# Cross-attention and expert layer on one core: batch 2's normalized input turned on TensorE, with new program orders on every engine

## The chip, the core and the metric

The kernel runs on one core of one Trainium2 chip. Five engines work side by side, each through its own list of instructions in order: TensorE (PE, matmuls), VectorE (DVE), ScalarE (ACT), GpSimd (POOL) and SyncE (SP), which here only issues DMAs. They wait for each other on semaphores. The metric is the device time of one execution in microseconds; lower is better.

## The reference, cut to what matters

```python
B, S, H = 4, 512, 512; T = 64; NH = 16; HD = 32; E = 8; K = 2; I = 16     # all float32
hs = layernorm(x)
q = clean(hs @ Wq.T + bq); k = clean(ctx @ Wk.T + bk); v = clean(ctx @ Wv.T + bv)
scores = clip(q @ k.T / sqrt(HD), -50, 50)
scores = clip(where(mask > 0.5, scores, -10000), -50, 50)
probs = softmax(scores); probs = probs / (probs.sum(-1) + 1e-8)
delta = clip(residual_scale, 0, 0.3) * ((probs @ v) @ Wo.T + bo)
x1 = x + layernorm(delta) * ln_gamma + ln_beta
n = layernorm(x1)
weights = softmax(x1 @ router_w.T)          # 8 experts, the two largest kept
a = silu(n @ down_w.T)                      # 8 experts x 16
out = x1 + sum over experts(gate * (a @ up_w.T))
```

The router, too, works on the normalized x1.

## The kernel before

A batch b (0 to 3) is 512 rows, in four tiles t of 128 rows. The program is a list of small steps, written out by hand for each engine in the order in which the engine runs them; a step named with (b, t) works on one tile, with (b, c), (b, m) or (b, r) on one chunk of the 512 columns or of the heads, with (b, j) or (b, g) on half a batch. There is no scheduler: an engine that reaches a step whose semaphore is not there yet stands, and all behind it stands too.

The steps of TensorE, with their lines in the kernel before (all products of two float32 operands that need accuracy are run as three passes of a high and a low part):

- `keys(c)`, `values(c)` (L522, L532): K and V of the context, one chunk of the weights each. They need the cleaned context chunk, counted by `ctx_ok`.
- `hs_transpose(b, t)` (L489): the normalized tile `hs` turned into a PSUM bank (uses h..). ScalarE then writes the high part (`hs_hi`, L748), VectorE the low part (`hs_lo`, L1089), which frees the bank.
- `query(b, m)` (L471, `hst`, `wq`): 12 matmuls of 512 columns. `query(b, 0)` waits for all four low parts of the batch. `query_out` (L771, ACT) takes it off.
- `scores(b, r)` (L548), `exp_scores` (L784, ACT), `clip` (L1148, DVE: the limits and the mask).
- `sums(b, g)` (L562): the softmax sums, 8 rows of which `reciprocals` (L1153, DVE) inverts; `spread_out` and `spread_in` send them to DRAM and back, spread over the partitions, into `wk`.
- `weigh(b, g)` (L575): probs times V; `product` (L1158, DVE) multiplies by the spread reciprocals; `att_hi` (L802, ACT) and `att_lo` (L1510, POOL) split it.
- `project(b, t)` (L471, `attt`, `wo`): 12 matmuls onto a bank in which `seed` (L845, ACT) has put the bias. Waits for the whole batch's `att_lo`.
- `projected_squares` (L854, ACT), `residual_powers` (POOL), `scaled` (L1167, DVE), `residual` (L1175, DVE), `x1_squares` (L862, ACT), `x1_powers` (POOL): the two layer norms.
- `down(b, t)` (8 matmul records of 136 columns each pass), `hid_transpose(b, j)`, `up(b, t)`: the experts; between them `down_scaled`, `hidden_tanh`, `exp_logits` (ACT), `rivals` (POOL), `largest`, `gating`, `hid_lo` (DVE), and at the end `finish` (L1224, DVE) and `store` (SP).

There are two ways to turn a tile. On TensorE as above, or moved: VectorE turns blocks of 32x32 (`hs_turn`, L1106; `x1_turn`, L1114), and two DMAs, out to DRAM and back in, put the blocks in place (`hs_send`, `hs_fetch`; `x1_send`, `x1_fetch`). `MOVED_HS` names the batches whose hs is moved (2 and 3 before), `MOVED` the halves whose x1 is moved (batches 0 to 2). For a moved batch the low part `hs_lo` is GpSimd's (L1516), for the others VectorE's.

The eight PSUM banks are dealt by the table `BANKS`: each line is a bank and the uses that follow each other in it. `take` makes TensorE wait until the use ahead in the same bank is freed. So `h11` behind `h10`'s bank mate, or `v10` behind `h..`, ties steps together.

At the start TensorE runs `WARM` = 18 matmuls on a constant tile while the first inputs land. SP issues all DMAs from one queue, in its written order; ahead of `x1_load` it waits until all four context chunks are cleaned (`clean_wait`, since the later loads `experts_load` and `bv_load` write over scratch that the cleaning reads). `load(2)` waits for both values to be complete (x of batch 2 takes the place of the value weights), `load(3)` for `wo_low(3)` (it takes that of the output weights).

## Time and profile before

| what | value |
|---|---|
| median of 3 runs | 198.33 us (197.42 to 199.66) |
| the profiled execution, its own time | 198.77 us |
| its span, first to last instruction | 197.1 us |
| TensorE busy | 178.3 us, 90% of the span |
| VectorE busy | 143.6 us, 73% |
| ScalarE busy | 112.5 us, 57% |
| GpSimd busy | 104.5 us, 53% |
| mean granted TensorE clock | 0.963 |

A busy share near 90% says that TensorE has work nearly always; what is left is the time in which it stood, and the time in which it ran at the lower of its two clock levels (0.50 in the profile is 1.2 GHz, 1.00 is 2.4 GHz). Matmul records overlap at their ends, so the distance from start to start is what one costs, not its own length.

### The profile page before, as it was taken

To read this page: it belongs to the slowest core of one execution; us is meant where nothing else is said; L and a number is where in the kernel's file an instruction comes from. 1 tells how busy PE (TensorE), PEld (TensorE's weight loads), DVE (VectorE), ACT (ScalarE), POOL (GpSimd) and SP (SyncE) were. 2 spreads that over 40 slices of the span, in tenths; PEclk is the share of its full clock that TensorE was granted. 3 is DMA by queue.
4 is the path that set the end of the run, shared out by engine and by line. 5 is a ranking of instruction groups with operands and counts; after the bars stand their busy time and mean duration, and the time that the engine had idled before them with its cause. 6 is when DMAs were issued, how large, how long until landed. Compare 5 with 4: busy or idle time off the path is not lost. (4 is left out here: it accounts for less than half of the span.)

```text
span 197.1 us, 3587 instructions
## 1 busy us (share of the span) xinstructions
PE 178.3 (90%) x1228; PEld 130.7 (66%) x1228; DVE 143.6 (73%) x306; ACT 112.5 (57%) x231; POOL 104.5 (53%) x157
## 2 busy tenths in 40 slices
PE   7999999399993999999599999986999999999970
PEld 7777686258832587885286876663775977888840
DVE  2867799999845894056982606789698999678991
ACT  3038537778309685175666833589554868567500
POOL 4060035499969999388694111794244872472000
PEclk9999999969998599999889999999999999999998
DMA  5994994005694326773305401553434482002337
GB/s 165 358 388 143 292 398 181 0 7 226 176 254 147 78 91 190 174 192 127 110 0 189 139 10 39 192 211 110 119 106 157 155 276 73 0 2 106 136 130 271
DMA packets 18050, 30.14 MB, mean 153 GB/s; under 512 B 3056, under 2 KB 8176, under 8 KB 17776
## 3 DMA queue, kind: packets, MB, share of 16 engines
q1 hardware_dynamic: 18032, 29.92, 46.6%
q8 instruction: 10, 0.16, 0.3%
q14 instruction: 8, 0.07, 0.1%
HBM read 19.95 MB, written 9.96 MB: 152 GB/s over the span
## 5 line engine op out<-in xcount | busy, mean ns | idle before, releaser
L471 PE MATMUL ps<-hst_hi,wq_hi 128*128 128x512 f32 x64 | 27.4, 428 | 0.0
L471 PE MATMUL ps<-hst_hi,wq_lo 128*128 128x512 f32 x64 | 26.4, 413 | 0.0
L471 PE MATMUL ps<-hst_lo,wq_hi 128*128 128x512 f32 x64 | 26.4, 412 | 0.0
L471 PE MATMUL ps<-wo_hi,attt_hi 128*128 128x512 f32 x64 | 26.1, 407 | 0.0
L471 PE MATMUL ps<-wo_hi,attt_lo 128*128 128x512 f32 x64 | 25.3, 395 | 0.0
L471 PE MATMUL ps<-wo_lo,attt_hi 128*128 128x512 f32 x64 | 25.2, 394 | 0.0
L1510 POOL TENSOR_TENSOR attt_lo<-wk,attt_hi 128x512 fp32r<-128x512 f32 x16 | 23.3, 1471 | 1.5 <-ACT attt_hi L802 1.5
L1506 POOL TENSOR_TENSOR xs<-xs,beta_bc 128x512 f32<-128x512 f32 x16 | 21.4, 1366 | 2.2 <-DMA beta_bc<-beta 2.2
L862 ACT ACTIVATE cen<-xs,n_sum 128x512 f32<-128x512 f32 x16 | 11.5, 721 | 15.5 <-DVE xs L1175 15.5
L1148 DVE TENSOR_SCALAR stage<-stage,exp_max 128x1024 f32<-128x1024 f32 x16 | 19.0, 1205 | 2.0 <-ACT stage L784 1.8
L765 ACT ACTIVATE hs<-xs,ln_bias,ln_rstd 128x512 f32<-128x512 f32 x16 | 12.1, 808 | 13.2 <-POOL ln_bias L1498 13.2
L1525 POOL TENSOR_SCALAR d_ve<-d_sq,rs_sq 128x1 f32<-128x1 f32 x16 | 5.9, 366 | 25.8 <-ACT cen L854 25.4
L1153 DVE RECIPROCAL rz<-ps 128x128 f32<-128x128 f32 x8 | 7.5, 952 | 15.4 <-PE ps L562 15.4
L771 ACT ACTIVATE q_sb<-ps,bq_sb 128x512 f32<-128x512 f32 x16 | 10.9, 684 | 13.1 <-PE ps L471 13.1
L1167 DVE TENSOR_TENSOR cen<-ps,gamma_bc 128x512 f32<-128x512 f32 x16 | 10.8, 677 | 10.1 <-ACT cen L854 10.1
L1175 DVE SCALAR_TENSOR_TENSOR xs<-cen,d_rstd,xs 128x512 f32<-128x512 f32 x16 | 14.1, 882 | 5.3 <-POOL d_rstd L1528 4.7
L471 PEld LDWEIGHTS ps<-dr_raw,x1t 128*128 128x128 f32 x128 | 15.5, 190 | 2.9 <-issue 2.2
L471 PEld LDWEIGHTS ps<-hst_hi,wq_hi 128*128 128x128 f32 x64 | 13.0, 202 | 6.4 <-issue 2.0
L784 ACT ACTIVATE stage<-ps 128x1024 f32<-128x1024 f32 x16 | 15.7, 1020 | 2.4 <-PE ps L548 2.4
L471 PE MATMUL ps<-dr_raw,x1t 128*128 128x136 f32 x128 | 16.6, 282 | 0.3 <-ACT x1t L748 0.2
L471 PEld LDWEIGHTS ps<-wo_hi,attt_hi 128*128 128x128 f32 x64 | 12.0, 188 | 5.6 <-issue 2.9
L854 ACT ACTIVATE cen<-ps 128x512 f32<-128x512 f32 x16 | 9.5, 591 | 10.3 <-PE ps L471 10.2
(111 smaller groups left out, 396.9 us busy)
## 6 DMA issues: line engine op xcount, KB each, us to landing
wk<-rz_scratch SPq DMA_DIRECT2D x32, 128.0 KB, 2.7
out<-xs SPq DMA_DIRECT2D x16, 256.0 KB, 2.3
xs<-x SPq DMA_DIRECT2D x3, 1024.0 KB, 7.8
x_scratch<-x_turned SPq DMA_DIRECT2D x6, 512.0 KB, 2.6
x_turned<-x_scratch SPq DMA_DIRECT2D x24, 128.0 KB, 2.7
hs_scratch<-hs_turned SPq DMA_DIRECT2D x2, 1024.0 KB, 3.8
hs<-hs_scratch SPq DMA_DIRECT2D x8, 256.0 KB, 5.2
wk<-wk_t SPq DMA_DIRECT2D x4, 256.0 KB, 5.9
```

The lines of the kernel that those rows point to most:

```text
L471: last = pe.matmul(dst, w, m, start=start and i == 0, stop=stop and i == n - 1, skip_group_check=unseen)
L765: act.activation(hs[:, t, :], xs[:, bass.ds(tile, 1), :], ACT.Identity, bias=ln_bias[:, bass.ds(tile, 1)], scale=ln_rstd[:, bass.ds(tile, ...
L771: act.activation(q_sb[:, m, :], bank(f"Q{b}{m}"), ACT.Identity, bias=bq_sb[:, m:m + 1]).then_inc(q_ok, 1)
L784: act.activation(probs[:, 2 * c:2 * c + 2, :], bank(f"S{b}{2 * c}", 2).rearrange("p (c n) -> p c n", c=2), ACT.Exp, scale=SCALE).then_inc( ...
L854: act.activation(cen[:, t, :], bank(f"W{b}{t}"), ACT.Square, accum_out=d_sq[:, NT * b + t:NT * b + t + 1]).then_inc(d_sq_ok, 1)
L862: act.activation(cen[:, t, :], xs[:, bass.ds(NT * b + t, 1), :], ACT.Square, bias=n_sum[:, NT * b + t:NT * b + t + 1], scale=-float(H), ac ...
L1148: dve.tensor_scalar(probs[:, ps, :], probs[:, ps, :], EXP_LO, exp_max[:, b:b + 1], ALU.max, ALU.min).then_inc(probs_ok, 1)
L1153: dve.reciprocal(rz[:, g, :], bank(f"s{b}{g}")[:, 0:P]).then_inc(sums_out, 1)
L1167: dve.tensor_tensor(cen[:, t, :], bank(f"W{b}{t}"), gamma_rs[:, :], ALU.mult).then_inc(w_free, 1)
L1175: dve.scalar_tensor_tensor(x_tile, cen[:, t, :], d_rstd[:, NT * b + t:NT * b + t + 1], x_tile, ALU.mult, ALU.add, accum_out=n_sum[:, NT * ...
L1506: pool.tensor_tensor(xt, xt, beta_bc[:, :], ALU.add).then_inc(xb_ok, 1)
L1510: pool.tensor_tensor(attt_lo[:, :, c, :], att[:, c, :].rearrange("p (t n) -> p t n", t=NT), attt_hi[:, :, c, :].bitcast(F32), ALU.subtract ...
```

## The change

`MOVED_HS` loses batch 2: its four tiles are now turned by `hs_transpose(2, 0)` to `(2, 3)` on TensorE and their low parts made by VectorE; `hs_turn`, `hs_send` and `hs_fetch` of batch 2 and GpSimd's four `hs_lo(2, t)` are gone. hs of batch 3 and x1 of batches 0 to 2 stay moved. `WARM` is 10 instead of 18. `clean_wait` is gone; its wait now stands in `experts_load`, and `x1_load`, `gamma_load`, `wo_load` and `bo_load` are issued ahead of it. `keys(0)` runs ahead of `values(0)`. The tables of banks and the order of steps on all five engines are new from there to the end. `weigh` gets one more wait, for the clipped probs that it reads. No step computes anything else than before.

```diff
-WARM = 18
+WARM = 10
-MOVED_HS = (2, 3,)
+MOVED_HS = (3,)
...
             def experts_load():
+                sp.wait_ge(ctx_ok, KC)
...
             small_load()
-            clean_wait()
             x1_load()
+            gamma_load()
+            wo_load()
+            bo_load()
+            experts_load()
             bv_load()
-            experts_load()
-            wo_load()
             load(2)
-            gamma_load()
-            bo_load()
-            hs_send(2)
+            load(3)
             spread_out(0, 0)
             spread_in(0, 0)
-            hs_fetch(2)
-            load(3)
             spread_out(0, 1)
...
             x1_send(0, 1)
+            hs_send(3)
             x1_fetch(0, 1)
+            hs_fetch(3)
             spread_out(2, 0)
             spread_in(2, 0)
+            x1_send(1, 0)
+            x1_send(1, 1)
+            x1_fetch(1, 0)
+            x1_fetch(1, 1)
             spread_out(2, 1)
             spread_in(2, 1)
...
                 if b == 0:
                     pe.wait_ge(values_out, 2)
+                pe.wait_ge(probs_ok, KC * b + 2 * g + 2)
...
+            keys(0)
             values(0)
-            keys(0)
             values(1)
             keys(1)
...
             query(0, 3)
-            scores(0, 0)
             hs_transpose(1, 0)
             hs_transpose(1, 1)
             hs_transpose(1, 2)
+            scores(0, 0)
             hs_transpose(1, 3)
+            expert_means()
+            query(1, 0)
+            sums(0, 0)
             scores(0, 1)
-            sums(0, 0)
-            query(1, 0)
+            weigh(0, 0)
             query(1, 1)
+            sums(0, 1)
+            scores(1, 0)
             query(1, 2)
             query(1, 3)
-            sums(0, 1)
-            weigh(0, 0)
-            scores(1, 0)
             weigh(0, 1)
-            expert_means()
+            sums(1, 0)
             scores(1, 1)
+            hs_transpose(2, 0)
+            hs_transpose(2, 1)
+            hs_transpose(2, 2)
+            project(0, 0)
+            project(0, 1)
+            project(0, 2)
+            sums(1, 1)
+            hs_transpose(2, 3)
+            project(0, 3)
             query(2, 0)
             query(2, 1)
             query(2, 2)
```

TensorE, in the program behind the last matmul of `query(0, 3)`. L548 is `scores`, L489 `hs_transpose`, L562 `sums`, L471 on `hst` `query`. Before:

```order
L471 MATMUL ps<-hst_hi,wq_lo 128x512
L548 MATMUL ps<-q_sb,k_sb 64x512 x8
L489 MATMUL ps<-ident,hs 128x128 x16
L548 MATMUL ps<-q_sb,k_sb 64x512 x8
L562 MATMUL ps<-stage,sum_ones 32x128 x16
L471 MATMUL ps<-hst_hi,wq_hi 128x512
```

The same place now (the lines are 4 lower: L544 is `scores`, L485 `hs_transpose`; L467 on `average` is `expert_means`):

```order
L467 MATMUL ps<-hst_hi,wq_lo 128x512
L485 MATMUL ps<-ident,hs 128x128 x12
L544 MATMUL ps<-q_sb,k_sb 64x512 x8
L485 MATMUL ps<-ident,hs 128x128 x4
L467 MATMUL ps<-dr_raw,average 128x136 x4
L467 MATMUL ps<-hst_hi,wq_hi 128x512
```

The first scores moved between the third and the fourth transpose of batch 1, `expert_means` came forward to here, and `scores(0, 1)` and `sums(0, 0)` went behind `query(1, 0)`.

VectorE, from the statistics of batch 2's tiles to the low parts of batch 1 (L1232 and L1234 are `tile_stats`, L1148 `clip`, L1089 `hs_lo`, L1249 `scale_gamma`). Before:

```order
L1249 TENSOR_SCALAR gamma_bc<-gamma_bc,rs_sb 128x512
L1232 BN_STATS ln_st<-xs 128x6
L1234 BN_AGGR ln_mv<-ln_st 128x2
L1148 TENSOR_SCALAR stage<-stage,exp_max 128x1024
L1089 TENSOR_TENSOR hst_lo<-ps,hst_hi 128x512 x3
L1148 TENSOR_SCALAR stage<-stage,exp_max 128x1024
L1089 TENSOR_TENSOR hst_lo<-ps,hst_hi 128x512
L1106 STREAM_TRANSPOSE hs_turned<-hs 128x4x4x32 x4
```

Now (L1241 to L1245 are `centre_wo`, L1090 `hs_lo`, L1149 `clip`):

```order
L1241 BN_STATS w_st<-xs 128x6
L1243 BN_AGGR w_mv<-w_st 128x2
L1245 TENSOR_SCALAR xs<-xs,w_mv 128x512
L1090 TENSOR_TENSOR hst_lo<-ps,hst_hi 128x512 x4
L1241 BN_STATS w_st<-xs 128x6
L1243 BN_AGGR w_mv<-w_st 128x2
L1245 TENSOR_SCALAR xs<-xs,w_mv 128x512
L1149 TENSOR_SCALAR stage<-stage,exp_max 128x1024 x2
```

The four low parts of batch 1 stand together and ahead of the first clips, two of the tile statistics of batch 2 moved behind them, and the four turns of batch 2 are gone.

SyncE, from the last small load to the first `spread_out`. Before (L305 is x of batch 1, L330 bv, L333 to L335 the experts, L314 Wo, L347 x of batch 2):

```order
L321 DMA rs_raw<-rs 128x1
L305 DMA xs<-x 128x4x512
L330 DMA hidden<-bv 128x512
L333 DMA dr_raw<-down_t 128x4x128
L334 DMA dr_raw<-router_t 128x4x8
L335 DMA hidden<-up_t 128x512
L314 DMA xs<-wo_t 128x4x512
L347 DMA xs<-x 128x4x512
L338 DMA gamma_bc<-gamma 128x512
L339 DMA beta_bc<-beta 128x512
L324 DMA bo_bc<-bo 128x512
L367 DMA hs_scratch<-hs_turned 128x2048
```

Now:

```order
L321 DMA rs_raw<-rs 128x1
L305 DMA xs<-x 128x4x512
L337 DMA gamma_bc<-gamma 128x512
L338 DMA beta_bc<-beta 128x512
L314 DMA xs<-wo_t 128x4x512
L324 DMA bo_bc<-bo 128x512
L332 DMA dr_raw<-down_t 128x4x128
L333 DMA dr_raw<-router_t 128x4x8
L334 DMA hidden<-up_t 128x512
L328 DMA hidden<-bv 128x512
L346 DMA xs<-x 128x4x512 x2
L352 DMA rz_scratch<-rz 128x128
```

Gamma, beta, Wo and bo moved ahead of the experts and bv, both x loads stand together, and the send of batch 2's turned hs is gone.

## Rows read from the trace of the kernel before

**Rows 1.** The page: busy times, and the granted clock in 40 slices.
```profile
PE 178.3 (90%) x1228; PEld 130.7 (66%) x1228; DVE 143.6 (73%) x306; ACT 112.5 (57%) x231; POOL 104.5 (53%) x157
PEclk9999999969998599999889999999999999999998
```

**Rows 2.** Waits of TensorE: line, op <- releaser: total us, times, longest.
```profile
PE ps L548 <- ACT stage L784: 3.3, 1, 3.3
PE ps L489 <- DVE hst_lo L1089: 3.2, 1, 3.2
PE ps L575 <- DVE wk L1158: 2.1, 1, 2.1
PE ps L489 <- DVE hidden L1215: 1.9, 2, 1.6
```

**Rows 3.** Timeline of TensorE: start us, us, line, operation, count [idle before].
```profile
1.05 6.12 PE L624 MATMUL ps<-average 128*128 128x128 f32 x36 [1.05 <-POOL average L1563]
...
22.43 0.51 PE L471 MATMUL ps<-hst_hi,wq_hi 128*128 128x512 f32 x1
...
33.79 1.11 PE L548 MATMUL ps<-q_sb,k_sb 32*64 32x512 f32 x16
34.84 1.53 PE L489 MATMUL ps<-ident,hs 128*128 128x128 f32 x12
39.59 1.09 PE L489 MATMUL ps<-ident,hs 128*128 128x128 f32 x4 [3.23 <-DVE hst_lo L1089]
40.61 1.99 PE L548 MATMUL ps<-q_sb,k_sb 32*64 32x512 f32 x16
...
63.47 2.01 PE L548 MATMUL ps<-q_sb,k_sb 32*64 32x512 f32 x16 [3.29 <-ACT stage L784]
65.41 0.80 PE L471 MATMUL ps<-hst_hi,wq_hi 128*128 128x512 f32 x1
...
69.82 0.39 PE L471 MATMUL ps<-hst_lo,wq_hi 128*128 128x512 f32 x1
```

**Rows 4.** Timeline of TensorE again, around the third stop.
```profile
96.28 1.26 PE L575 MATMUL ps<-stage,v_sb 64*32 64x512 f32 x16 [2.13 <-DVE wk L1158]
97.46 0.79 PE L471 MATMUL ps<-hst_hi,wq_hi 128*128 128x512 f32 x1
...
100.56 0.39 PE L471 MATMUL ps<-hst_lo,wq_hi 128*128 128x512 f32 x1
```

**Rows 5.** Timeline of VectorE: cleaning, clips, and a product behind its spread.
```profile
4.86 0.45 DVE L1275 COPY_PREDICATED compare<-dr_raw,stage 128x256 f32<-128x256 uint8 x1
...
48.78 3.48 DVE L1148 TENSOR_SCALAR stage<-stage,exp_max 128x1024 f32<-128x1024 f32 x2
...
66.64 1.29 DVE L1158 TENSOR_TENSOR wk<-ps,wk 128x512 f32<-128x512 f32 x2 [0.47 <-DMA wk<-rz_scratch]
```

**Rows 6.** Groups by line: operation, count | busy us, mean ns | idle before.
```profile
L1510 POOL TENSOR_TENSOR attt_lo<-wk,attt_hi 128x512 fp32r<-128x512 f32 x16 | 23.3, 1471 | 1.5 <-ACT attt_hi L802 1.5
L1148 DVE TENSOR_SCALAR stage<-stage,exp_max 128x1024 f32<-128x1024 f32 x16 | 19.0, 1205 | 2.0 <-ACT stage L784 1.8
L1089 DVE TENSOR_TENSOR hst_lo<-ps,hst_hi 128x512 fp32r<-128x512 f32 x8 | 5.3, 686 | 2.5 <-ACT hst_hi L748 2.4
L1106 DVE STREAM_TRANSPOSE hs_turned<-hs 128x512 f32<-128x512 f32 x8 | 5.0, 672 | 0.0
```

**Rows 7.** SyncE's DMA issues: start us, us of issuing, line, transfer, count.
```profile
46.09 0.33 SPq L353 DMA_DIRECT2D rz_scratch<-rz  x1
49.26 1.72 SPq L361 DMA_DIRECT2D wk<-rz_scratch  x4
...
62.46 1.72 SPq L361 DMA_DIRECT2D wk<-rz_scratch  x4
```

**Rows 8.** Busy us of each engine (instructions) in one stretch, granted clock, DMA share, GB/s.
```profile
140.00:190.00 50.00, 49.37 (x320) 39.21 (x319) 42.80 (x120) 31.30 (x85) 21.73 (x42) 1.00 0.35 116
```

**Rows 9.** The last row of the chain that ended last: start us, us, what.
```profile
192.05 0.60 DVE xs L1224
```

More of the change, by code:

```diff
@@ new lines, in _ @@
+            x1_squares(0, 3)
+            query_out(2, 1)
+            query_out(2, 2)
+            x1_out(0, 0)
+            att_hi(1, 0)
+            att_hi(1, 1)
+            exp_scores(2, 0)
+            down_scaled(0, 0)
+            exp_scores(2, 1)
+            x1_out(0, 1)
+            att_hi(1, 2)
+            att_hi(1, 3)
+            query_out(2, 3)
+            x1_out(0, 2)
+            x1_out(0, 3)
+            seed(1, 0)
+            exp_scores(2, 2)
+            down_scaled(0, 1)
@@ L1342, in _ @@
             hs_lo(1, 2)
+            hs_lo(1, 3)
+            centre_wo(3)
+            clip(0, 0)
             clip(0, 1)
-            hs_lo(1, 3)
-            hs_turn(2, 0)
-            hs_turn(2, 1)
-            hs_turn(2, 2)
-            hs_turn(2, 3)
+            tile_stats(2, 2)
             reciprocals(0, 0)
-            centre_wo(2)
-            centre_wo(3)
+            tile_stats(2, 3)
             clip(0, 2)
+            centre_experts()
             clip(0, 3)
             centre_bo()
+            tile_stats(3, 0)
@@ L1367, in _ @@
+            clip(1, 2)
+            clip(1, 3)
+            hs_lo(2, 0)
             hs_turn(3, 0)
+            scaled(0, 0)
+            hs_lo(2, 1)
+            hs_lo(2, 2)
+            scaled(0, 1)
             hs_turn(3, 1)
             hs_turn(3, 2)
-            hs_turn(3, 3)
-            clip(1, 2)
-            clip(1, 3)
-            reciprocals(1, 0)
+            residual(0, 0)
             reciprocals(1, 1)
-            scaled(0, 0)
-            residual(0, 0)
-            x1_turn(0, 0)
@@ L1378, in _ @@
-            scaled(0, 1)
+            hs_lo(2, 3)
             residual(0, 1)
-            x1_turn(0, 1)
             scaled(0, 2)
             residual(0, 2)
+            scaled(0, 3)
+            x1_turn(0, 0)
+            x1_turn(0, 1)
+            x1_turn(0, 2)
+            residual(0, 3)
+            x1_turn(0, 3)
+            hs_turn(3, 3)
             product(1, 0)
             product(1, 1)
-            scaled(0, 3)
-            residual(0, 3)
-            product(1, 2)
             clip(2, 0)
@@ L1418, in _ @@
+            hid_lo(0, 0)
+            clip(3, 0)
+            clip(3, 1)
+            largest(0, 1)
+            gating(0, 1)
+            reciprocals(3, 0)
+            product(2, 2)
+            product(2, 3)
+            largest(1, 0)
             clip(3, 2)
             clip(3, 3)
-            largest(0, 1)
-            hid_lo(0, 0)
-            reciprocals(3, 1)
+            product(3, 0)
+            product(3, 1)
             scaled(2, 0)
             residual(2, 0)
-            gating(0, 1)
+            x1_turn(2, 0)
@@ L1426, in _ @@
             scaled(2, 1)
+            reciprocals(3, 1)
             residual(2, 1)
-            x1_turn(2, 0)
+            finish(0, 0)
+            finish(0, 1)
             x1_turn(2, 1)
+            gating(1, 0)
             hid_lo(0, 1)
             scaled(2, 2)
-            product(3, 0)
-            product(3, 1)
             residual(2, 2)
```

462 lines of the change are left out of this document (208 added, 254 removed), and 16 rows, old and new, of the table BANKS.

## The prediction

> **What bounds the kernel now.** The page comes first: TensorE is busy 178.3 of 197.1 us, and its granted clock falls in three places of the 40 slices [rows 1]. So the time is TensorE's work, plus the stretches where it stands, plus what the lower clock costs behind them. TensorE's waits name the stops: three of 3.3, 3.2 and 2.1 us, and two short ones of 1.9 us together [rows 2]. Its timeline shows where they lie and what follows each. I price them from start to start:
>
> - Full rate: `query(0, 0)` to `(0, 3)` take 22.43 to 33.79, 11.36 us for 48 matmuls, 0.237 us each; one `scores` takes 33.79 to 34.84, 1.05 us; twelve transposes take 1.53 us, 0.13 us each [rows 3].
> - Stop A: `hs_transpose(1, 3)` stands 3.23 us for VectorE's low part of tile (1, 0), whose bank it needs. The clock is then at its lower level (1.2 GHz): four transposes take 39.59 to 40.61, 1.02 for 0.52, and `scores(0, 1)` about 1.94 for 1.05 (that is what the other `scores` at this level takes, 63.47 to 65.41) [rows 3]. 3.2 + 0.5 + 0.9 = 4.6 us.
> - Stop B: `scores(1, 1)` stands 3.29 us for the exponentials, which on ScalarE are queued behind four `hs_hi(2, t)` that wait for batch 2's hs to come back from DRAM. Then the `scores` loses 0.9 us, and ten matmuls take 65.41 to 69.82, 4.41 for 2.37 [rows 3]. 3.3 + 0.9 + 2.0 = 6.2 us.
> - Stop C: `weigh(1, 1)` stands 2.13 us for a product, and seven matmuls then take 97.46 to 100.56, 3.10 for 1.66 [rows 4]. 2.1 + 1.4 = 3.6 us with rounding.
>
> Together 14.4 us, which an order that fits better can give back. From 140 to 190 us TensorE is busy 49.37 of 50 and VectorE 42.80 [rows 8]: little can be had there, and VectorE is close to being the bound itself.
>
> **The change, part by part.**
>
> *The beginning.* The warm-up with the 36 records of 18 matmuls runs from 1.05 for 6.12 us [rows 3]; the first context chunk is clean at 4.86 + 0.45 = 5.3 [rows 5]. Eight matmuls fewer end it at about 5.3, so TensorE starts `keys(0)` 1.7 us earlier. A few tenths are lost again, because the first transposes now come before ScalarE's second tile is ready. I take 1.4 us (bounds 0.8 and 1.7): `query(0, 0)` at 21.0 for 22.4. The earlier x1, gamma and Wo loads only keep this up: by my count VectorE ends the low parts of batch 0 at 20.8 and four statistics of 0.85 at 24.2; GpSimd, which first adds beta four times (1.4 us each, from about 19.5), has the scales at 27; ScalarE, between other steps, has the tiles normalized by 31.6, and TensorE asks for them at 32.3. That is little cover: GpSimd later by over 1 us shows on TensorE.
>
> *Stop A goes.* `scores(0, 0)` now stands between the third and fourth transpose, and the four low parts of 0.69 us [rows 6] ahead of the clips. The first is done at about 34.3, TensorE asks at 34.7. `query(1, 0)` needs the fourth, at about 36.7, and `expert_means` ends at 36.1: 0.6 us of new wait.
>
> *Stop B goes, clips and products come in its place.* ScalarE no longer waits for batch 2's round trip. But between `hs_lo(1, 3)` and `clip(1, 1)` VectorE has a `centre_wo`, six clips, six tile statistics, two reciprocals, `centre_experts`, `centre_bo`, gamma and two products. With clips at their mean of 1.2 us [rows 6] that is 18.9 us of work, and 0.8 of waits puts it at 56.3. TensorE in the same stretch has four queries (11.4), two `scores`, two `weigh`, two `sums` and short waits, and asks for `clip(1, 1)` at about 55.0. Two clips with GpSimd busy took 3.48 us, 1.74 each [rows 5]; at that price six of them are 3.2 us longer. I take 1.1 of it: the wait of `sums(1, 0)` is 2.4, and `sums(0, 0)` and `(0, 1)` wait 1.0 together (bounds 2.0 and 5.5 for the three).
>
> The Trainium skill (SBUF — State Buffer, "Who interferes with whom") says that a VectorE operation in a two-port mode and a GpSimd operation shut each other out for a whole instruction. The long clips agree. By that rule, with a GpSimd operation of about 1.4 us ahead of each clip, the six would cost some 8 us more and not 1.1, and the sum would come to about +1.
>
> *Transposes of batch 2.* Sixteen at 0.13 us are 2.0 us more on TensorE [rows 3]. VectorE gives four turns of 0.67 us for four low parts of 0.69 [rows 6], nothing; GpSimd loses four low parts; the send and four fetches leave SP's queue. The banks of these transposes hang on the products: h20 needs `product(0, 2)`, h21 `product(0, 3)`, h22 a reciprocal. A product comes 7.4 us after its reciprocal: 3.2 from the send to the fetch (46.09 to 49.26) and 4.2 from the fetch to the product (62.46 to 66.64) [rows 5, 7]. `reciprocals(0, 1)` ends at about 50.6 (36.6, then `centre_wo` 1.4, four clips 4.8, four statistics 3.4, two reciprocals 1.8, two centrings 2.0, waits 0.6), so `product(0, 2)` is at 58 to 59, and TensorE arrives at 58.4 to 59.5. Behind `product(0, 3)` come two `att_hi` of 0.6 and two `att_lo` of 1.47 us on GpSimd [rows 6] before `project(0, 0)` may start. I count 2.5 us here (bounds 1 and 5).
>
> *Stop C goes.* `weigh(1, 1)` finds its products made. In its place `down(0, 0)` stands right behind `scores(2, 0)` and needs x1 of batch 0 back from DRAM: about 0.9 us. Two more small ones, `weigh(2, 1)` behind `down_scaled` and `up(1, 0)` behind a low part, are 0.8.
>
> *The last third.* The short stops of 1.9 us [rows 2] go, since `hid_transpose(0, 0)` has more work ahead of it. TensorE arrives about 6 us earlier, but VectorE's work there is the same, and it was 86% busy [rows 8]: transposes and downs of batches 2 and 3 in turn wait for banks. I add 1.0 net (bounds 0 and 5). The tail from the last `finish` (192.05 + 0.60, then the store) [rows 9] stays at 4.5 us.
>
> *The clock.* Several waits now lie together between 55 and 62 us. Before, it fell after each of the three stops of over 2 us and after none of the short ones. I add 0.8 us, a third to a half of what it cost behind A, B or C (1.4 to 2.9).
>
> The sum: −1.4 (beginning) −4.6 −6.2 −3.6 (stops A, B, C) −1.9 (short stops) +2.0 (transposes) +0.6 +2.4 +1.0 +2.5 +0.9 +0.8 (new waits, 8.2) +0.8 (clock) +1.0 (last third) = −5.7 us. The span goes from 197.1 to 191.4. The profiled execution took 198.77, 0.4 above the median of 198.33; against the median the forecast is 192.6 us.
>
> **The rivals.**
>
> *More comes back.* If clips run at the mean and the last third keeps pace, 2.4 falls to 1.3, and the clock, last-third and part of the product terms vanish: 3 to 4 us more, about 189. For it: the new order has work ahead of each old stop. Against: VectorE's share at the end.
>
> *The clock falls in the new cluster, and clips are slow.* Then the waits at 55 to 62 cost 2.9 like B's clock loss and 2 us more of clips: +4, 196.6. The Trainium skill (TensorE: Matmul & The Clock Gate, "PE-mode transpose") says that transposes on TensorE do not count as busy for its clock gate; by that the twelve of batch 2, each behind a wait, would bring the clock down at `project(0, 0)`, with the same 196.6. Against it: the twelve at 34.84 ran at full rate, 0.13 us each [rows 3].
>
> *Slower: the reciprocals of batch 2 stuck in SP's queue.* `spread_out(2, 1)` is now behind two sends and eight fetches of x1 of batch 1, the second send waiting for `x1_turn(1, 3)`. From that turn it is 2.6 us for the send, 3.5 for the fetches, then 7.4 for the spread: 13.5 us until `product(2, 2)`, which frees the bank of `weigh(3, 0)`. TensorE has about 13 us of work between. So this place has no slack, and every us by which VectorE's turn is late is a us of standing, and 2 us for the clock on top. It decides from 6 us of lateness: −5.7 + 6 + 2 is 200.6, 1% above before. For it: VectorE is the bound of the first 60 us, too; against it: TensorE and VectorE slip together there.
>
> *Nothing changes:* the waits only move, all new ones at their upper bounds (+3, +2.5, +4) against −5.7: about 198 to 202.
>
> **How the numbers follow.** The forecast, 190 to 195.5 around 192.6, gets 0.55; more comes back (below 190) 0.15; clock and clips (195.5 to 197.5) 0.15; nothing changes (197.5 to 200.3) 0.06; the stuck queue or another late chain (above) 0.09. A measurement of this kernel tells 1% from no change, 196.35 to 200.31. Faster: 0.55 + 0.15 + half of 0.15 is 0.78; same 0.12; slower 0.10. The range that leaves out less than 2 in 10 is 188.5 to 198.0; the likeliest case's own is 190 to 195.5.
>
> **What would show it.** `query(0, 0)` starts at 21 us and `query(1, 0)` before 38. No stop of TensorE over 3 us; its waits name `clip`, products and `attt_lo` between 50 and 64 us, in all 4 to 7 us, and the granted clock falls at most once there. `project(2, 0)` starts some 7 us earlier than before. The transposes of hs are 48, at 0.13 us from start to start. I am wrong if the waits of the middle exceed 10 us, if ScalarE's order, which I followed only along TensorE's needs, holds a wait that I do not see, or if the last third loses more than 5 us to VectorE.

## The result and the profile after

The changed kernel takes 189.55 us (median of 4 runs, 189.04 to 191.93); before stands at 198.26 us in the same comparison. The ratio is 0.9545 [0.9475, 0.9616], 8.7 us less. The forecast was 192.6 us with 188.5 to 198.0, so the time lies in the range, but where the rival "more comes back" was put (below 190). The ratios, here and in the table below, leave out executions more than 1.5% above the fastest of the same kernel; the medians hold all of them.

The first profile of the changed kernel is of its longest execution, in which the clock fell twice. The rows below are of the same kernel, run again: 190.21 us, span 188.4, mean clock 1.000. On the page the busy time of TensorE and the granted clock in 40 slices answer to [rows 1]:

```profile
PE 173.6 (92%) x1228; PEld 127.4 (68%) x1228; DVE 140.2 (74%) x306; ACT 113.8 (60%) x231; POOL 98.8 (52%) x153
PEclk9999999999999999999999999999999999999999
```

TensorE's waits answer to [rows 2] (total us, times, longest):

```profile
PE ps L544 <- ACT q_sb L772: 1.7, 1, 1.7
PE ps L467 <- POOL attt_lo L1511: 1.3, 1, 1.3
```

Its timeline over the places of stops A and B and the new cluster answers to [rows 3] (L621 the warm-up, L528 `values`, L518 `keys`, L485 transposes, L544 `scores`, L558 `sums`, L467 the rest):

```profile
1.05 4.40 PE L621 MATMUL ps<-average 128*128 128x128 f32 x20 [1.05 <-POOL average L1564]
...
9.54 1.98 PE L528 MATMUL ps<-xs,compare 128*128 128x512 f32 x4 [0.65 <-DMA xs<-wv_t]
11.93 1.99 PE L518 MATMUL ps<-compare,wk 128*128 128x256 f32 x8 [0.41 <-DMA wk<-wk_t]
...
33.69 1.47 PE L485 MATMUL ps<-ident,hs 128*128 128x128 f32 x12
35.09 1.11 PE L544 MATMUL ps<-q_sb,k_sb 32*64 32x512 f32 x16
36.79 0.63 PE L485 MATMUL ps<-ident,hs 128*128 128x128 f32 x4 [0.58 <-DVE hst_lo L1090]
37.29 1.19 PE L467 MATMUL ps<-dr_raw,average 128*128 128x136 f32 x8
38.96 0.47 PE L467 MATMUL ps<-hst_hi,wq_hi 128*128 128x512 f32 x1 [0.48 <-DVE hst_lo L1090]
...
42.53 1.08 PE L558 MATMUL ps<-stage,sum_ones 128*32 128x128 f32 x32 [0.54 <-DVE stage L1149]
...
58.60 1.11 PE L544 MATMUL ps<-q_sb,k_sb 32*64 32x512 f32 x16
60.17 1.22 PE L485 MATMUL ps<-ident,hs 128*128 128x128 f32 x8 [0.46 <-DVE wk L1159]
61.64 0.63 PE L485 MATMUL ps<-ident,hs 128*128 128x128 f32 x4 [0.24 <-DVE rz L1154]
63.52 0.47 PE L467 MATMUL ps<-wo_hi,attt_hi 128*128 128x512 f32 x1 [1.25 <-POOL attt_lo L1511]
```

The fourth transpose of batch 1 waits 0.58 us where stop A was 3.23. `scores(1, 1)` at 58.60, where stop B was, and `weigh(1, 1)`, where stop C was, do not wait at all. The waits in front of `project(0, 0)` are 0.46, 0.24 and 1.25, and the clock stays at 1.00 behind them.

**Where the 8.7 us are.** The profiled spans are 197.1 and 188.4. TensorE's busy time fell by 4.7 us (178.3 to 173.6). That is 1.7 less warm-up (6.12 to 4.40), 2.1 more for the 16 transposes, and so, by difference, 5.1 for the lower clock that is gone. The stops inside TensorE's list, those of over 0.15 us added up, fell from 11.7 to 9.4: −2.3. From TensorE's last matmul to the end it was 5.95 us and is 4.09: −1.9, and of this 1.6 is the last stores of that one execution of before, which landed late. The last `finish` ended 4.45 us before the end there and 2.8 to 2.9 us before it in the experiments on before below. So TensorE's part is about 7 us in this pair, and the clock is the larger share of it. The medians are 8.7 us apart as well, but each profiled execution is slower than its median, by 0.5 and 0.7 us, and the late stores belong to one execution; so about 1.6 us of the difference of the medians is not in this account and stays open.

Times and clocks of single executions give a second estimate. In 27 executions of before, the mean clock went from 0.952 (spans 197.2 to 199.2) to 0.989 (194.5). A straight line through them gives 0.97 us per 0.01, and 193 at full clock; single executions lie up to 2.2 us off it. The changed kernel has 0.996 or more in seven of its eight executions. By that line about 3 us of the 8.7 are clock, by the busy times above 5; I take it as 3 to 5. That is an estimate: an execution that stands longer also has the lower clock, so the line cannot tell the two apart.

### The profile page after: what moved, and what is told of

Its sections match the earlier page's. It is cut to its first block, busy times and chain, and to the rows that moved or that the text cites. A ratio compares the mean times of both kernels' runs of the same rounds, so it can differ in the third digit from the quotient of the medians.

```text
span 190.1 us, 3580 instructions
## 1 busy us (share of the span) xinstructions
PE 176.2 (93%) x1228; PEld 128.9 (68%) x1228; DVE 140.2 (74%) x306; ACT 113.9 (60%) x231; POOL 98.6 (52%) x153
## 4 chain that ended last, share of the span: by engine, by line
PE 15%; DMA 13%; DVE 12%; issue 6%; SPq 5%; ACT 4%; POOL 4%; DVEq 0%; ACTq 0%
PE ps L467 11%; DMA x_scratch<-x_turned 4%; DMA wk<-rz_scratch 4%; DMA x_turned<-x_scratch 3%; SPq L381 3%; DVE xs L1225 3%; DMA rz_scratch<-rz 2%; PE ps L572 2%; POOL d_rstd L1529 2%; DVE x_turned L1115 2%; SPq L360 1%; PE ps L544 1%; DVE xs L1176 1%; PE ps L558 1%; DVE cen L1168 1%
## 5 line engine op out<-in xcount | busy, mean ns | idle before, releaser
L1511 POOL TENSOR_TENSOR attt_lo<-wk,attt_hi 128x512 fp32r<-128x512 f32 x16 | 20.3, 1282 | 17.4 <-ACT attt_hi L803 17.4
L467 PE MATMUL ps<-wo_hi,attt_hi 128*128 128x512 f32 x64 | 25.9, 405 | 1.2 <-POOL attt_lo L1511 1.2
L467 PE MATMUL ps<-hst_hi,wq_hi 128*128 128x512 f32 x64 | 26.5, 414 | 0.3 <-DVE hst_lo L1090 0.3
L467 PE MATMUL ps<-hst_lo,wq_hi 128*128 128x512 f32 x64 | 25.7, 402 | 0.0
L467 PE MATMUL ps<-hst_hi,wq_lo 128*128 128x512 f32 x64 | 25.4, 397 | 0.0
L467 PE MATMUL ps<-wo_hi,attt_lo 128*128 128x512 f32 x64 | 25.3, 395 | 0.0
L467 PE MATMUL ps<-wo_lo,attt_hi 128*128 128x512 f32 x64 | 25.2, 394 | 0.0
L467 PEld LDWEIGHTS ps<-dr_raw,x1t 128*128 128x128 f32 x128 | 15.6, 190 | 3.8 <-issue 2.7
L467 PE MATMUL ps<-dr_raw,x1t 128*128 128x136 f32 x128 | 16.5, 282 | 0.6 <-DVE hidt_lo L1090 0.4
L863 ACT ACTIVATE cen<-xs,n_sum 128x512 f32<-128x512 f32 x16 | 11.5, 722 | 9.2 <-DVE xs L1176 9.1
L772 ACT ACTIVATE q_sb<-ps,bq_sb 128x512 f32<-128x512 f32 x16 | 10.9, 683 | 10.1 <-PE ps L467 10.0
L1149 DVE TENSOR_SCALAR stage<-stage,exp_max 128x1024 f32<-128x1024 f32 x16 | 14.3, 922 | 3.5 <-ACT stage L785 3.5
L467 PEld LDWEIGHTS ps<-hst_hi,wq_hi 128*128 128x128 f32 x64 | 12.4, 194 | 6.0 <-issue 2.7
L1159 DVE TENSOR_TENSOR wk<-ps,wk 128x512 f32<-128x512 f32 x16 | 10.3, 682 | 8.0 <-PE ps L572 4.2
L1176 DVE SCALAR_TENSOR_TENSOR xs<-cen,d_rstd,xs 128x512 f32<-128x512 f32 x16 | 13.2, 828 | 3.1 <-POOL d_rstd L1529 2.8
L803 ACT CAST attt_hi<-wk 128x512 fp32r<-128x512 f32 x16 | 9.7, 616 | 9.4 <-DVE wk L1159 7.3
L467 PEld LDWEIGHTS ps<-wo_hi,attt_hi 128*128 128x128 f32 x64 | 12.0, 188 | 4.2 <-issue 1.8
L467 PEld LDWEIGHTS ps<-hst_hi,wq_lo 128*128 128x128 f32 x64 | 12.3, 193 | 2.9
L467 PEld LDWEIGHTS ps<-hst_lo,wq_hi 128*128 128x128 f32 x64 | 12.3, 193 | 2.5
```

What stands on the lines that cost most here:

```text
L467: last = pe.matmul(dst, w, m, start=start and i == 0, stop=stop and i == n - 1, skip_group_check=unseen)
L772: act.activation(q_sb[:, m, :], bank(f"Q{b}{m}"), ACT.Identity, bias=bq_sb[:, m:m + 1]).then_inc(q_ok, 1)
L803: act.copy(attt_hi[:, :, c, :], att[:, c, :].rearrange("p (t n) -> p t n", t=NT)).then_inc(attt_hi_ok, 1)
L863: act.activation(cen[:, t, :], xs[:, bass.ds(NT * b + t, 1), :], ACT.Square, bias=n_sum[:, NT * b + t:NT * b + t + 1], scale=-float(H), ac ...
L1149: dve.tensor_scalar(probs[:, ps, :], probs[:, ps, :], EXP_LO, exp_max[:, b:b + 1], ALU.max, ALU.min).then_inc(probs_ok, 1)
L1159: dve.tensor_tensor(att[:, c, :], bank(f"v{b}{c}"), att[:, c, :], ALU.mult).then_inc(weighed_out, 1)
```

## The experiments

The first four run or edit the changed kernel, the next four edit the kernel before, the last four the changed kernel again. Medians are of 4 runs (one of 10); before is 198.7, 198.3 and 197.5 us in the three groups. A dash says that no ratio is on record.

| kernel | us | ratio to before |
|---|---|---|
| changed, again | 189.47 (188.06 to 190.43) | 0.9537 [0.9464, 0.961] |
| changed, hs of batch 2 moved | 196.63 (192.21 to 198.49) | – |
| changed, transposes of batch 2 twice | 189.70 (189.46 to 191.33) | 0.9572 [0.9507, 0.9636] |
| changed, WARM 18 | 189.76 (188.53 to 190.24) | 0.9547 [0.9486, 0.9609] |
| before, low parts first | 200.83 (199.4 to 201.12) | 1.0154 [1.007, 1.0238] |
| before, fetch first | 196.58 (193.62 to 198.21) | – |
| before, both | 200.06 (199.3 to 201.23) | 1.0135 [1.0042, 1.0228] |
| before, WARM 10 | 195.49 (193.91 to 198.2) | 0.9872 [0.9758, 0.9986] |
| changed, query_out first | 189.47 (189.21 to 190.1) | 0.9613 [0.9554, 0.9672] |
| changed, load(3) later | 192.80 (191.71 to 194.59) | 0.9756 [0.9692, 0.982] |
| changed, all three | 193.74 (191.29 to 196.62) | 0.9741 [0.9653, 0.9829] |
| changed, moved, filled | 196.71 (193.77 to 198.51) | 0.986 [0.9801, 0.992] |

### The changed kernel again

> The changed kernel again, as the yardstick of this chip for the three runs beside it. Both theories: 189.5 us, within 0.7 us. Its traces so far had stops of TensorE of 2.0 us ahead of scores(3, 0) and 1.9 us ahead of hs_transpose(1, 3); where the clock falls behind them it is 2 us longer.

189.47 us; its rows are above. The time repeats.

### hs of batch 2 moved again

```diff
-MOVED_HS = (3,)
+MOVED_HS = (2, 3,)
...
             spread_out(0, 1)
             spread_in(0, 1)
+            hs_send(2)
             spread_out(1, 0)
+            hs_fetch(2)
             spread_in(1, 0)
...
-            hs_transpose(2, 0)
-            hs_transpose(2, 1)
-            hs_transpose(2, 2)
             project(0, 0)
...
-            hs_transpose(2, 3)
             project(0, 3)
```

with the low parts of batch 2 still VectorE's, and the steps of batches 2 and 3 on ScalarE, VectorE and GpSimd put where the new order has room.

> The changed kernel with hs of batch 2 turned by VectorE and two DMAs again, its low parts still VectorE's; hs_norm(3), hs_hi(2), hs_lo(2) and hs_turn(3) had to be put where this leaves no circle of waits. Theory of the order (the gain is that of stops removed by new orders, and the transposes themselves only cost TensorE 2.0 us): 187.5 to 189.5 us, since the round trip of 12 us fits behind project(0, 0) to (0, 2). Rival, the gain comes from the round trip that is no longer there: 192 us or more, with a stop of over 2 us ahead of query(2, 0).

196.63 us, 7.2 more in the median. All four executions (192.21 to 198.49) lie above all of the changed kernel's, so it is slower; how much by is less sure. The rival's time has come, but not its place: the stop ahead of `query(2, 0)` is 0.62 us, not over 2. TensorE's timeline, and two 5-us stretches (busy us of PE, PEld, DVE, ACT, POOL, then clock, DMA share, GB/s):

```profile
63.60 0.76 PE L469 MATMUL ps<-wo_hi,attt_hi 128*128 128x512 f32 x1 [3.66 <-POOL attt_lo L1513]
...
79.15 0.47 PE L469 MATMUL ps<-hst_hi,wq_hi 128*128 128x512 f32 x1 [0.62 <-DVE hst_lo L1096]
...
92.80 2.15 PE L469 MATMUL ps<-dr_raw,x1t 128*128 128x136 f32 x8 [2.73 <-ACT x1t L809]
```
```profile
60.00:65.00 5.00, 1.40 (x3) 1.16 (x4) 3.81 (x5) 4.84 (x8) 2.49 (x2) 0.68 0.65 236
65.00:70.00 5.00, 5.00 (x16) 3.94 (x15) 0.24 (x1) 0.94 (x3) 0.17 (x1) 0.64 1.00 231
```

`project(0, 0)` starts at 63.60, as with the transposes (63.52). The transposes cost nothing in that place: without them TensorE stands there. But a stop of 3.66 us stands where twelve transposes were, and the clock falls. From `project(0, 0)` to `query(2, 0)` it is 15.55 us for 12.83. Then x1 of batch 0 comes late (2.73 us at `down(0, 0)`). One execution of this kernel kept a clock of 0.999 and took 192.21 us. Read so, of the 7.2 us some 2.7 are stops and delays and some 4.4 clock; that is an estimate that leans on a single execution.

### The transposes of batch 2 twice

```diff
-                for c in range(len(src)):
+                for c in list(range(len(src))) * (2 if use[:2] == "h2" else 1):
```

> The changed kernel with each of the sixteen transposes of batch 2 run twice into the same place, the result unchanged. If the transposes lie on TensorE's path as my sum has it: +2.0 us. If the wait of project(0, 0) for att_lo (1.24 us, behind three of the four tiles) takes them up: +0.8 us. If they are hidden: 0.

189.70 us, +0.2, within the scatter: the third case. The timeline shows where twelve of the second sixteen went:

```profile
59.99 2.81 PE L485 MATMUL ps<-ident,hs 128*128 128x128 f32 x24 [0.22 <-DVE wk L1159]
63.34 0.47 PE L467 MATMUL ps<-wo_hi,attt_hi 128*128 128x512 f32 x1 [0.54 <-POOL attt_lo L1511]
```

Twelve more transposes there, and the wait behind them falls from 1.25 to 0.54: they lie beside GpSimd's `att_lo`. With sixteen transposes or with thirty-two, `project(0, 0)` waits for `att_lo` (it starts at 63.34 us for 63.52). The steps ahead of `att_lo` are reciprocals, round trip, `product` and `att_hi`.

### WARM 18 in the changed kernel

```diff
-WARM = 10
+WARM = 18
```

> The changed kernel with 18 warm-up matmuls for 10. My sum: +1.4 us. Rival: the start is bound by the loads of Wv and Wk and by the low parts of batch 0 (TensorE stood 0.4, 0.4 and 0.35 us for them), so that query(0, 0) starts where it did: 0 to +0.5 us.

189.76 us, +0.3, within the scatter: the rival.

```profile
23.25 0.47 PE L467 MATMUL ps<-hst_hi,wq_hi 128*128 128x512 f32 x1
...
58.87 1.08 PE L558 MATMUL ps<-stage,sum_ones 128*32 128x128 f32 x32 [1.32 <-DVE stage L1149]
...
63.55 0.47 PE L467 MATMUL ps<-wo_hi,attt_hi 128*128 128x512 f32 x1 [1.10 <-POOL attt_lo L1511]
```

`query(0, 0)` starts 0.8 later (22.45 with 10), `project(0, 0)` at the same time. The beginning has slack against the same chain. The 1.32 us at `sums(1, 0)` are new. They come from the two clips ahead, which start at 56.30 and take 2.42 us here, where GpSimd's `att_lo` starts at 56.52; in the changed kernel they start at 55.72 and take 1.41, and `att_lo` starts at 56.47.

### Before, low parts of batch 1 first (the edit of stop A alone)

```diff
-            scores(0, 0)
             hs_transpose(1, 0)
             hs_transpose(1, 1)
             hs_transpose(1, 2)
+            scores(0, 0)
             hs_transpose(1, 3)
+            query(1, 0)
             scores(0, 1)
             sums(0, 0)
-            query(1, 0)
```

with the four `hs_lo(1, t)` ahead of `scale_gamma`, two tile statistics and the first clip on VectorE, and on ScalarE `exp_scores(0, 0)` behind `hs_hi(1, 2)` and `hs_hi(1, 3)` ahead of `exp_scores(0, 1)`.

> The kernel before with the edit for its first stop alone: scores(0, 0) between the third and fourth transpose of batch 1, the low parts of batch 1 ahead of the clips, query(1, 0) ahead of scores(0, 1). If each stop is worth what I priced it at: -4.6 us, 193.7. Rival: batch 2's round trip through DRAM starts no earlier, so the second stop grows by what the first gives back: 0 to -2 us, and the stop ahead of scores(1, 1) is 5 us or more.

200.83 us, slower by 1.5%.

```profile
37.73 0.63 PE L489 MATMUL ps<-ident,hs 128*128 128x128 f32 x4 [0.74 <-DVE hst_lo L1089]
39.90 0.47 PE L471 MATMUL ps<-hst_hi,wq_hi 128*128 128x512 f32 x1 [1.55 <-DVE hst_lo L1089]
...
48.44 0.51 PE L471 MATMUL ps<-hst_hi,wq_hi 128*128 128x512 f32 x1 [1.91 <-ACT stage L784]
...
66.50 2.02 PE L548 MATMUL ps<-q_sb,k_sb 32*64 32x512 f32 x16 [4.21 <-ACT stage L784]
```

Stop A (3.23) becomes two of 0.74 and 1.55, and the clock falls behind them all the same (0.68 and 0.50 from 40 to 44 us). Then `query(1, 1)` waits for an exponential to free its bank, and stop B grows from 3.29 to 4.21. The rival had this growth (to 5 or more), but not that the whole would be slower. Stop C stays (2.17).

### Before, fetch first (stop B alone)

```diff
             spread_out(0, 0)
-            spread_in(0, 0)
             hs_fetch(2)
+            spread_in(0, 0)
```

> The kernel before with one edit in the queue of loads: hs_fetch(2) ahead of spread_in(0, 0). If the second stop is bound by where the fetch stands in the queue: hs_hi(2, 0) starts at 54.8 us for 58.7, the stop ahead of scores(1, 1) goes, -4 to -6 us. If it is bound by the round trip itself or by the query before it: less than 1 us.

196.58 us, 1.7 less than before in the same group where 4 to 6 were expected, and within the scatter of both. Stop B is gone: `scores(1, 1)` runs at 61.57 without a wait. So B was SyncE's order, with batch 2's fetch queued behind the spread of the sums, and not the way of turning as such. But 30 us later:

```profile
91.33 1.12 PE L548 MATMUL ps<-q_sb,k_sb 32*64 32x512 f32 x16 [1.92 <-DVE cen L1167]
94.61 1.96 PE L575 MATMUL ps<-stage,v_sb 64*32 64x512 f32 x16 [2.16 <-DVE wk L1158]
```

A new stop of 1.92 us stands ahead of stop C. C stays, and so does the lower clock there.

### Before, both edits

> Both edits. If the stops add up: -9 us, 189.5, with no transposes of batch 2 on TensorE at all. If the round trip bounds: -2 to -5 us.

200.06 us, slower by 1.4%. The stops are now 2.35 (`weigh(0, 1)`), 2.56 (`scores(2, 0)`) and 2.15 (`weigh(1, 1)`): three of over 2 us again. The effects of the two edits do not add: −9 us was the sum.

### Before, WARM 10

```diff
-WARM = 18
+WARM = 10
```

> The kernel before with 10 warm-up matmuls for 18. My sum: -1.4 us. Rival, loads and low parts bound the start: 0, and query(0, 0) starts at 22.4 as before.

195.49 us, 0.9872 [0.9758, 0.9986]: 2.8 us less in the median, twice what I had put on it. The start of `query(0, 0)` moved by 0.3 us only (22.12), but the fourth transpose of batch 1 then waited 1.59 us in place of 3.23, and the clock did not fall there; stop B was longer (4.07). The profiled execution is the slowest of the four (198.2), so it does not show where the median got its 2.8 us. By the medians the old order gets about a third of the 8.7 us from this edit alone, and the changed kernel next to nothing (0.3, within the scatter). The cause of the shorter stop A stays open: it was 3.23 and 3.29 in the other two profiles with the old order at that place, but in the changed kernel the same wait changes from one execution to another (below).

### The changed kernel, query_out(3, 1) first

```diff
             query_out(3, 0)
+            query_out(3, 1)
             x1_squares(1, 3)
             att_hi(2, 1)
-            query_out(3, 1)
```

In the changed kernel ScalarE's rows show why `scores(3, 0)` waits 1.73 us at 115.80: the second copy of the query (L772) stands behind `x1_squares` (L863), which waits for VectorE.

```profile
111.70 0.67 ACT L772 ACTIVATE q_sb<-ps,bq_sb 128x512 f32<-128x512 f32 x1
113.84 0.72 ACT L863 ACTIVATE cen<-xs,n_sum 128x512 f32<-128x512 f32 x1 [1.47 <-DVE xs L1176]
...
115.07 0.68 ACT L772 ACTIVATE q_sb<-ps,bq_sb 128x512 f32<-128x512 f32 x1
```

> The changed kernel with one step moved: ScalarE does query_out(3,1) ahead of x1_squares(1,3) and att_hi(2,1). In the changed kernel scores(3,0) starts at 115.80 us after a stop of 1.73 us for the query of batch 3, whose copy stands in ScalarE's row behind x1_squares(1,3), and that one waits for VectorE's residual(1,3). Theory (the stop is made by the order of ScalarE alone): the stop is gone, scores(3,0) starts by 114.2, and the time falls by 1 to 1.7 us, to some 188.2. Rival (what follows waits for its own inputs): the microsecond comes back before weigh(3,0), where products are waited for already (1.02 us), and the time stays within 0.4 us of 189.5.

189.47 us: the rival. `scores(3, 0)` starts at 112.90 with no wait, and eight microseconds on:

```profile
121.46 1.17 PE L467 MATMUL ps<-dr_raw,x1t 128*128 128x136 f32 x8 [2.44 <-ACT x1t L811]
```

`down(1, 0)` needs x1 of batch 1. It starts 1.0 us earlier than in the changed kernel (122.47), but this whole execution is 1.1 us ahead from `project(0, 0)` on (62.41 for 63.52), so x1 is no earlier by the edit. The whole 1.73 us and more stands there (0.55 before the edit), and the clock falls behind it.

### The changed kernel, load(3) behind the spreads

In the changed kernel the first product of the second half waits for its reciprocals to come back (VectorE), and SyncE's rows show the 1 MB of x of batch 3 (L346) issued just ahead of the first round trip (L352 out, L360 back), then the second one:

```profile
55.72 1.41 DVE L1149 TENSOR_SCALAR stage<-stage,exp_max 128x1024 f32<-128x1024 f32 x2
59.34 1.29 DVE L1159 TENSOR_TENSOR wk<-ps,wk 128x512 f32<-128x512 f32 x2 [2.22 <-DMA wk<-rz_scratch]
```
```profile
43.54 0.38 SPq L346 DMA_DIRECT2D xs<-x  x1
44.65 0.34 SPq L352 DMA_DIRECT2D rz_scratch<-rz  x1
50.44 1.74 SPq L360 DMA_DIRECT2D wk<-rz_scratch  x4
52.33 0.34 SPq L352 DMA_DIRECT2D rz_scratch<-rz  x1
54.67 1.70 SPq L360 DMA_DIRECT2D wk<-rz_scratch  x4
```

```diff
             load(2)
-            load(3)
             spread_out(0, 0)
             spread_in(0, 0)
             spread_out(0, 1)
             spread_in(0, 1)
+            load(3)
...
-            centre_bo()
-            tile_stats(3, 0)
-            tile_stats(3, 1)
             reciprocals(0, 1)
-            tile_stats(3, 2)
-            tile_stats(3, 3)
+            centre_bo()
...
             product(0, 3)
+            tile_stats(3, 0)
+            tile_stats(3, 1)
+            tile_stats(3, 2)
+            tile_stats(3, 3)
             reciprocals(1, 0)
```

and on GpSimd `batch_power(3)` behind the four `att_lo(0, c)`.

> The changed kernel with load(3), 1 MB of x, issued in SP's row behind the two round trips of batch 0's sums instead of ahead of them; in VectorE's row reciprocals(0,1) stands ahead of centre_bo and tile_stats(3,0..3) behind product(0,3), and in GpSimd's batch_power(3) behind att_lo(0,3). In the changed kernel product(0,2) waits 2.22 us for the spread reciprocals and starts at 59.34 us, and project(0,0) starts at 63.52 after waiting for GpSimd's att_lo of that tile's batch. Theory (the chain sums, round trip, product, att_lo sets project(0,0), and the transfer of x ahead in the queues makes the round trip 5.8 us long): the round trip falls to some 3.5 us, project(0,0) starts at 61.3 to 61.8, and the time falls by 1.5 to 2 us, to some 187.7. Rival (the chain is not what bounds, or x of batch 3 comes late): project(0,0) moves and the gain is given back by the time of down(0,0), or in a wait for transposes or squares of batch 3; the time stays within 0.4 us of 189.5.

192.80 us, 3.3 more. The first leg of the first round trip, from issue to issue, is 3.00 us for 5.79, and `product(0, 2)` starts at 57.01 for 59.34.

```profile
43.82 0.33 SPq L352 DMA_DIRECT2D rz_scratch<-rz  x1
46.82 1.73 SPq L360 DMA_DIRECT2D wk<-rz_scratch  x4
50.05 0.34 SPq L352 DMA_DIRECT2D rz_scratch<-rz  x1
51.61 1.70 SPq L360 DMA_DIRECT2D wk<-rz_scratch  x4
```

But the two are not cause and effect, as I had taken it. `product(0, 2)` needs the second round trip, and that one goes out when `reciprocals(0, 1)` is done, in both kernels: it ends at 52.30 in the changed kernel (start 51.37, behind statistics) and the send is issued at 52.33; here it ends at 50.02, since it was moved ahead of the statistics, and the send is issued at 50.05. So the 2.3 us go with VectorE's part of the edit, not with the place of the load; and `product(0, 2)` then waits 0.52 us for TensorE's `weigh`, no longer for the transfer.

```profile
60.27 0.69 DVE L1233 BATCH_NORM_STATS2 ln_st<-xs 128x6 f32<-128x512 f32 x1 [1.98 <-DMA xs<-x]
...
63.49 0.92 DVE L1154 RECIPROCAL rz<-ps 128x128 f32<-128x128 f32 x1
```
```profile
64.56 0.80 PE L485 MATMUL ps<-ident,hs 128*128 128x128 f32 x4 [4.63 <-DVE rz L1154]
```

But the statistics of batch 3 now wait for x, which comes late, and `reciprocals(1, 0)` is queued behind them. It frees the bank of `hs_transpose(2, 2)`, so TensorE stands 4.63 us. What I had placed behind a wait was worse than the wait. `reciprocals(0, 1)` moved forward alone, with `load(3)` left where it was, is the edit that these rows suggest; it was not run.

### The changed kernel, three edits

The two before, with `hs_lo(1, t)` ahead of `centre_wo(2)`, `wo_high(2)` behind `exp_scores(0, 1)`, and `wo_low(2)` behind `add_beta(1, 3)`.

> The changed kernel with the edits of the two runs before it in this list together, and the low halves of batch 1 on VectorE ahead of centre_wo(2), with wo_high(2) on ScalarE behind exp_scores(0,1), and wo_low(2) on GpSimd one step later. Theory (the stops of TensorE that remain lie on one path and add): the 0.5 us ahead of query(1,0), some 2 us ahead of project(0,0) and some 1.5 us ahead of scores(3,0) go, and the time is 185.5 to 186.5. Rival (they share a slack, as the edits of the kernel before did when made one by one): not better than the better of the two edits alone.

193.74 us: it inherits the stop of the edit before (3.32 us ahead of the third transpose of batch 2), has the x1 wait of 2.54 us, and adds one of 2.00 us at `sums(0, 0)`, which waits for its clips. The forecast of 185.5 to 186.5 is missed by 7 us. None of my edits beat the changed kernel.

### Moved, with the gap filled

```diff
+            def filler():
+                pe.wait_ge(weighed_out, banks.count("v02"))
+                for i in range(12):
+                    pe.transpose(bank("v02")[:, (i % 4) * P:(i % 4 + 1) * P], ident[:, :], ident[:, :])
...
             scores(1, 1)
+            filler()
             project(0, 0)
```

This is against the kernel with hs of batch 2 moved. The filler turns the unit matrix twelve times; its result is not used.

> The kernel in which hs of batch 2 is moved by the DMA queues again (196.63 us), with 12 transposes of the unit matrix put on TensorE between scores(1,1) and project(0,0), where the changed kernel has the transposes of batch 2 for 12 of its 16. They write a bank that nobody reads then and are extra work, not part of the computation. In the kernel without them project(0,0) starts at 63.60 us after a stop of 3.66 us, the clock is lower behind it, and query(2,0) starts at 79.15 us where the changed kernel has 76.35. Theory (the stop lets the clock fall, and any work of TensorE in it, transposes too, holds it up): project(0,0) stays at 63.6, query(2,0) starts near 76.5, and the time falls by some 2.8 us, to 193.8. Rival one (transposes do not hold the clock up): query(2,0) stays near 79.2 and the time near 196.6. Rival two (it is the wait for x1 before down(0,0) that carries the time): query(2,0) moves but down(0,0) stays near 92.8 and the time within 1 us of 196.6.

196.71 us over 10 runs, no change in the median. The expected 2.8 us are missed, though the profiled execution, one of the faster (193.95), shows the local effect:

```profile
59.08 1.53 PE L593 MATMUL ps<-ident 128*128 128x128 f32 x12
62.51 0.47 PE L469 MATMUL ps<-wo_hi,attt_hi 128*128 128x512 f32 x1 [1.91 <-POOL attt_lo L1519]
...
75.77 0.47 PE L469 MATMUL ps<-hst_hi,wq_hi 128*128 128x512 f32 x1 [0.61 <-DVE hst_lo L1102]
...
89.40 2.15 PE L469 MATMUL ps<-dr_raw,x1t 128*128 128x136 f32 x8 [2.71 <-ACT x1t L815]
```
```profile
60.00:65.00 5.00, 3.09 (x17) 2.43 (x16) 2.72 (x3) 4.15 (x7) 2.26 (x2) 1.00 0.68 217
```

The clock there is 1.00 for 0.68, and `project(0, 0)` to `query(2, 0)` is 13.26 us for 15.55. But x1 of batch 0 comes late as before, the clock falls at `down(0, 0)`, and the ten executions have mean clocks from 0.960 to 0.991. That x1 is late is at least in part my placement: the send of its first half is issued at 81.89 us (79.35 in the changed kernel), behind a block of four `hs_norm(3, t)` of 2.94 us on ScalarE. So this pair does not price the moved round trip cleanly. It shows that filling the one stop does not give the 7 us back in the median.

## Why the prediction was right, and where it was off

**Stops A, B, C: right.** All three are gone with their clock losses (14.4 us forecast). The experiments on before add what the sum could not. The low parts break stop A into two, one line in SyncE's queue removes stop B, and the time is then given back at the next places, all of it for A and most of it for B. No edit removed C alone. I read this as a gain of the new order as a whole; it is an inference, since no run has the new order with everything else left as it was. What the turning of batch 2 on TensorE gives in it would be fewer transfers in SyncE's queue, and work for TensorE in a place where it stands otherwise; only the second is shown (63.60 and 63.52). How it would do in before's order alone was not run.

**The beginning: the step failed.** −1.4 was forecast; `query(0, 0)` starts at 22.45 in place of 22.43. The eight matmuls are gone (−1.7), but TensorE then waits 0.65 and 0.41 us for the value and key weights. From start to start these two places cost 0.8 and 0.7 us, nearly the whole 1.7. The warm-up had covered the arrival of the weights, which the working left out. Nothing was lost by it in the end, as WARM 18 shows (+0.3).

**Transposes and the cluster at `project(0, 0)`: two terms that were one.** 2.0 + 2.5 was forecast; transposes and waits measure 2.1 + 1.95. The size is right, but adding them was wrong in principle: doubling the transposes costs 0.2 and removing those in front of it moves `project(0, 0)` by 0.1. They fill the wait for `att_lo`.

**Clips at `sums(1, 0)`: 2.4 forecast, none seen.** The six clips ahead took 0.7 to 0.75 us each (1.41 for two at 55.72), not the 1.2 of the mean or the 1.74 of [rows 5]. Two of them, at 45.8 and 47.2, have only short steps of GpSimd beside them. A `wo_lo` of GpSimd that began at 41.79, during the two clips of 40.98, took 1.72 us; the two at 37.01, beside VectorE's low parts, took 1.26 each. Next to `att_lo` the clips are slow here too: the two at 62.24 took 2.23 us. With WARM 18, where the last two of the six began 0.6 us later, they took 2.42 us and `sums(1, 0)` waited 1.32. So the term was not baseless; that it came out at nothing hung on a few tenths of a microsecond. In these rows the duration of an operation goes with the neighbour it has, not with the group's mean: L1149 measures 916 ns, L1148 of before 1205 [rows 6]. The rule of the Trainium skill on shared ports (SBUF — State Buffer, "Who interferes with whom"), by which the clips would have cost 8 us more, did not come to bear on these six clips: I had assumed a long GpSimd operation ahead of each, and there was none.

**`down(0, 0)` 0.9: none. `query(1, 0)` and its transpose 0.6: 1.06. `sums(0, 0)` and `(0, 1)` 1.0: 0.54. `weigh(2, 1)` and `up(1, 0)` 0.8: 0.85.** Together 3.3 were forecast and 2.45 measured. The short stops (1.9) are gone, as forecast.

**The clock +0.8: nothing.** I expected one fall in the cluster. None came in any profile of the changed kernel, its repeat, or its variants with WARM 18 and doubled transposes, at that place. The rival by which transposes do not hold the clock fell with it: in the 3.8 us from the end of `scores(1, 1)` at 59.7 to 63.52 TensorE did only twelve transposes, and the clock stayed at 1.00; with nothing in that place for 3.66 us it was lower behind it (0.68 from 60 to 65 us). The Trainium skill (TensorE: Matmul & The Clock Gate, "PE-mode transpose") says that transposes do not count as busy in the same way. The rows here speak against it for float32 transposes, also with 24 of them at 59.99, and with the filler of the last experiment, in one profiled execution each.

**The queue of SyncE for batch 2 (rival, 200.6): its place is real, its price small.** `weigh(3, 0)` waits for the products of batch 2:

```profile
130.16 1.09 PE L572 MATMUL ps<-stage,v_sb 64*32 64x512 f32 x16 [1.02 <-issue]
```

The view names no engine here; VectorE's two products of batch 2 start at 129.37 us, after 2.18 us of waiting for their reciprocals, and take 0.65 each, so the first ends about when `weigh(3, 0)` starts. It is 1.0 us in place of 6. **Not foreseen:** the 1.73 us at `scores(3, 0)`, a ScalarE row that I had followed only along TensorE's needs, as the text had warned, and 0.55 at `down(1, 0)`.

**The last third, +1.0: about nothing.** After `project(2, 0)` (133.35) TensorE's waits are 0.42, 0.24 and 0.39. `project(2, 0)` is 3.9 us earlier than before and not 7, partly since `weigh(3, 0)` and two downs now come ahead of it.

In sum, TensorE's last matmul ends 6.8 us earlier in the profiled pair for 5.7 forecast. The further 1.9 are the shorter end, of which 1.6 was an accident of the one execution against which the sum was made. That the first two numbers are so near is in part luck. The beginning (1.4), `scores(3, 0)` (1.7), `weigh(3, 0)` (1.0) and `down(1, 0)` (0.55) went against the sum; the clips (2.4), `down(0, 0)` (0.9), the clock (0.8) and most of the last third (1.0) went for it. What came is nearer to the rival "more comes back" (0.15) than to the main case, in its time and in what it named: quick clips, no fall of the clock, a last third that keeps pace.

Of the signs, three came: no stop of over 3 us (the longest is 1.73, and 2.01 in the first profile), no more than one fall of the clock between 50 and 64 us (none), transposes at 0.12 to 0.13 us. Four did not: `query(0, 0)` at 21 (22.45), `query(1, 0)` before 38 (38.96), 4 to 7 us of waits between 50 and 64 (1.95), `project(2, 0)` 7 us earlier (3.9).
